# A two-layer cross network on Trainium2: layer 1 multiplies by x after the matmul instead of before it

## The reference

```python
e = stack([tbl_f[ids[:, f]] for f in range(32)], axis=1)    # (512, 32, 32)
prev = x0 = e
for W in (filter_0, filter_1):     # (1, 32*32, 128), (1, 32*128, 128)
    z = einsum('bhd,bmd->bhmd', x0, prev).reshape(b, h * m, d)
    prev = relu(einsum('bpd,pn->bnd', z, W[0]))
    outs.append(prev)
z = sum(concatenate(outs, axis=1), axis=-1)                 # (512, 256)
h = relu(concatenate([z, dense_ctx], axis=1) @ W_top1 + b_top1)
h = relu(h @ W_top2 + b_top2)
y = h @ W_top3
```

## Time and profile before

| | us |
|---|---|
| median of 3 runs | 1014.08 (1012.17 to 1014.36) |
| span of the profiled execution | 1007.7 |
| median less span | 6.4 |
| PE busy | 926.3 |
| DVE busy | 900.1 |
| POOL busy | 799.1 |
| ACT busy | 494.0 |
| mean granted clock of TensorE | 0.995 |

### The profile page before, as it was taken

How to read it: one execution, slowest core, us unless ns; L and a number is a source line. 1 busy time by engine, 2 the same in 40 slices (tenths; PEclk the granted TensorE clock), 3 DMA queues, 4 the chain that set the end, 5 groups by cost and what they waited for, 6 DMA issues and landing times.

```text
span 1007.7 us, 11260 instructions
## 1 busy us (share of the span) xinstructions
PE 926.3 (92%) x3132; PEld 590.2 (59%) x3132; DVE 900.1 (89%) x750; ACT 494.0 (49%) x606; POOL 799.1 (79%) x461
## 2 busy tenths in 40 slices
PE   0168899999999999999999999999999999999998
PEld 0125466666656666666656666666666666666664
DVE  0128999999899999999899999999999999999971
ACT  0224555556455545556445455556555555454531
POOL 6727988987997999987997999987877767777760
PEclk9999999999999999999999999999999999999999
DMA  8178556555565555555564555455555545555100
GB/s 230 37 218 263 172 182 186 180 185 162 142 197 167 191 183 186 165 179 172 154 195 157 190 191 186 145 193 171 163 193 183 193 162 187 184 159 172 42 0 0
DMA packets 58645, 166.70 MB, mean 165 GB/s; under 512 B 9649, under 2 KB 23185, under 8 KB 50466
## 3 DMA queue, kind: packets, MB, share of 16 engines
q1 hardware_dynamic: 51602, 160.62, 49.2%
q0 software_dynamic: 4096, 2.11, 1.5%
q10 hardware_dynamic: 2928, 3.76, 1.2%
HBM read 129.75 MB, written 5.24 MB: 134 GB/s over the span
## 4 chain that ended last, share of the span: by engine, by line
PE 61%; issue 16%; DVE 14%; DMA 4%; ACT 4%; SPq 1%; DVEq 0%; ACTq 0%
PE acc L814 26%; PE acc L751 11%; PE acc L753 11%; PE acc L752 11%; DVE prod L692 7%; DVE lo L644 5%; ACT hi L509 3%; DMA prev_rep<-prev 2%; DVE prod L648 2%; DMA whole<-xt_scratch 1%; DMA ctx_in<-in_dense_ctx 1%; PE prev_ps L851 1%; ACT relu L574 1%; PE acc L766 0%; PE prod L843 0%
## 5 line engine op out<-in xcount | busy, mean ns | idle before, releaser
L406 POOL TENSOR_TENSOR whole<-xa,prev_rep 128x1024 f32<-128x1024 f32 x224 | 541.3, 2421 | 137.3 <-PE acc L814 115.2
L509 ACT ACTIVATE hi<-prod 128x1024 fp32r<-128x1024 f32 x352 | 360.5, 1026 | 392.4 <-DVE prod L692 250.4
L644 DVE TENSOR_TENSOR lo<-prod,hi 128x1024 fp32r<-128x1024 f32 x352 | 417.2, 1221 | 20.7 <-ACT hi L509 19.1
L814 PE MATMUL acc<-whole,w_whole 128*128 128x512 f32 x896 | 420.6, 592 | 0.0
L751 PE MATMUL acc<-hi,w_hi 128*128 128x512 f32 x704 | 367.7, 522 | 29.8 <-DVE lo L644 17.3
L692 DVE TENSOR_TENSOR prod<-xa,prev_ps 128x1024 f32<-128x1024 f32 x288 | 339.9, 1221 | 0.6
L753 PE MATMUL acc<-hi,w_lo 128*128 128x512 f32 x704 | 279.2, 397 | 0.0
L752 PE MATMUL acc<-lo,w_hi 128*128 128x512 f32 x704 | 276.5, 393 | 0.0
L814 PEld LDWEIGHTS acc<-whole,w_whole 128*128 128x128 f32 x896 | 168.9, 188 | 125.5 <-issue 107.6
L751 PEld LDWEIGHTS acc<-hi,w_hi 128*128 128x128 f32 x704 | 134.0, 190 | 113.8 <-issue 56.5
L752 PEld LDWEIGHTS acc<-lo,w_hi 128*128 128x128 f32 x704 | 134.3, 191 | 71.5 <-issue 50.4
(11 more groups left out here) (60 smaller groups left out, 204.3 us busy)
## 6 DMA issues: line engine op xcount, KB each, us to landing
xa<-xt_scratch SPq DMA_DIRECT2D x32, 2048.0 KB, 7.6
prev_rep<-prev SPq DMA_DIRECT2D x128, 256.0 KB
xb<-xt_scratch SPq DMA_DIRECT2D x30, 1024.0 KB
x<-xt_scratch SPq DMA_DIRECT2D x62, 192.0 KB
xm<-xt_scratch SPq DMA_DIRECT2D x31, 256.0 KB
xt_scratch<-xt_stage SPq DMA_DIRECT2D x7, 256.0 KB
whole<-in_L_rec_filter SPq DMA_DIRECT2D x18, 64.0 KB
xt_scratch<-xt_stage SPq DMA_DIRECT2D x9, 128.0 KB
```

Source lines behind the costliest of these rows:

```text
L406: pool.tensor_tensor(whole[:, k % R], xa[:, par, g:g + 2, :], prev_rep[:, par, j, None, :].to_broadcast([P, 2, C]), ALU.mult).then_inc(who ...
L509: act.activation(hi[:, slot], prod[:, n_prod % 2], ACT.Copy).then_inc(hi_ready, 1)
L644: dve.tensor_tensor(lo[:, slot], prod[:, n_prod % 2], hi[:, slot].bitcast(F32), ALU.subtract).then_inc(lo_ready, 1)
L814: mm = pe.matmul(acc1[:], w1_whole[:, m, u, :], whole[:, m % R, u, :], start=False, stop=m == WHOLES - 1 and u == 1)
```

## The change

Layer 1 is turned round. The stationary operand is now a slice of `prev` (128 maps m by the 128 examples of one d, `prev_hi` and `prev_lo`, split once per chunk from the PSUM of layer 0), and the moving operand is the filter of four fields at a time (`w1_hi`, `w1_lo`, 128 rows m by 4 fields times 128 outputs). The result has the examples on the partitions, and x[b, h, d] is one number per partition and field, which scales it afterwards.

A chunk has four tiles q (one d each), a tile has eight PSUM banks of four fields, and each bank is three fp32r matmuls. For four of the eight banks ("A", `bank_a`, PSUM `ya`, 2 banks) ACT scales each field's 128 columns from PSUM into `scaled` (`scale_bank`, four ACTIVATEs with a per-partition scale read from `emb`), and POOL adds the four banks up in two additions (`sum_tile`, 1024 and 512 columns). For the other four ("D", `bank_d`, PSUM `yd`, 3 banks) DVE multiplies and adds field by field onto a running sum in SBUF that starts from POOL's part (`add_bank`, four `scalar_tensor_tensor` of 128 columns). DVE then folds the sum over the last four fields and takes the relu and the sum over d (`finish_a`, `finish_b`, `finish_c`).

Nothing is replicated any more: `replicate_prev`, `xa`, `acc1`, the fp32 matmuls and the copies of `prev` to PSUM are gone. Layer 0 keeps its 13 matmuls, one K-tile at a time with one `prod` bank; `xm` is copied to PSUM by ACT (`copy_xm`), so that DVE's product has one operand there. DVE takes over `sum0`. The chunks are software-pipelined and written out, no longer in hardware loops: iteration c of eight slots runs `bank_a` of chunk c, `bank_d` of chunk c - 1 and layer 0 of chunk c + 1, and there are 33 iterations. Batch tile 1's first 16 gathers are ahead of the loop, the rest inside it, and `emb` has two slots. The core of the diff (removed code of the old layer 1 is shown only in part):

```diff
...
+    DB = 4
+    AB = F // HB - DB
+    A_FIELD = HB * DB
+    RD, RA = 3, 2
+    PR = 3
...
-        acc1 = psum("acc1", [P, C])
-        prev_ps = psum("prev_ps", [P, 2, C])
-        prod = psum("prod", [P, 2, 2, C])
+        prod = psum("prod", [P, C])
+        xm_ps = psum("xm_ps", [P, C])
+        yd = psum("yd", [P, RD, C])
+        ya = psum("ya", [P, RA, C])
         identity = sb("identity", [P, P])
...
-            def replicate_prev(q):
-                for j in range(J):
-                    part = prev[32 * j:32 * (j + 1), q, :]
-                    src = bass.AP(part.tensor, part.offset, [list(part.ap[0]), [0, 4], [1, C]])
-                    sp.dma_start(prev_rep[:, q, j, :], src).then_inc(prev_replicated[q][j], 16)
...
+            def sum_tile(c, q):
+                n = DC * c + q
+                pool.wait_ge(a_used, a_number(c, q, AB - 1) + 1)
+                if n > 0:
+                    pool.wait_ge(part_ready, n)
+                piece = scaled[:, n % PR, :]
+                pool.tensor_tensor(half[:], piece[:, 0:AB * C // 2], piece[:, AB * C // 2:AB * C], ALU.add).then_inc(halved, 1)
+                if c > 1:
+                    pool.wait_ge(d_used, d_number(c - 2, q, 0) + 1)
+                pool.wait_ge(halved, n + 1)
+                pool.tensor_tensor(part[:, c % 2, q].rearrange("p i n -> p (i n)"), half[:, 0:C], half[:, C:2 * C],
+                                   ALU.add).then_inc(part_ready, 1)
...
+            for c in range(CHUNKS):
+                some = gathers_of(c)
+                for q in range(DC):
+                    sum_tile(c, q)
+                    for bt, f in some[len(some) * q // DC:len(some) * (q + 1) // DC]:
+                        if f == 0 and bt >= 2:
+                            pool.wait_ge(d_used, DB * DC * CPB * (bt - 1))
+                        gather(bt, f, gathered[bt])
+                    if q == 0 and c + 1 < CHUNKS:
...
+            def split_high(c, k):
+                n = KT * c + k
                 act.wait_ge(product_ready, n + 1)
-                act.activation(hi[:, slot], prod[:, n_prod % 2], ACT.Copy).then_inc(hi_ready, 1)
+                if n > 1:
+                    act.wait_ge(split_used, n - 1)
+                act.activation(hi[:, n % 2, :], prod[:], ACT.Copy).then_inc(hi_ready, 1)
...
+            def prev_high(c):
...
+                act.activation(prev_hi[:, c % 3, :], acc0[:], ACT.Relu).then_inc(prev_hi_ready, 1)
+            def scale_bank(c, q, j):
+                n, tile = a_number(c, q, j), DC * c + q
+                act.wait_ge(a_ready, n + 1)
+                if j == 0 and tile >= PR:
+                    act.wait_ge(halved, tile - PR + 1)
+                for i in range(HB):
+                    op = act.activation(scaled[:, tile % PR, C * j + N * i:C * j + N * (i + 1)],
+                                        ya[:, n % RA, N * i:N * (i + 1)], ACT.Copy,
+                                        scale=scale_of(c, q, A_FIELD + HB * j + i))
+                op.then_inc(a_used, 1)
             act.wait_ge(gathered_first, 16 * EARLY)
...
+                for s in range(SLOTS):
+                    if turning and s == TURN_SLOT:
+                        stage_xt((c + TURN_LEAD) // CPB, 0)
+                        stage_xt((c + TURN_LEAD) // CPB, 1)
+                    for j in (2 * (s % 2), 2 * (s % 2) + 1):
+                        scale_bank(c, s // 2, j)
+                        if j % 2 == 0 and c + 1 < CHUNKS:
+                            if s < KT:
+                                split_high(c + 1, s)
+                            if s == KT:
+                                small_high(c + 1)
+                            if s == 6:
+                                prev_high(c + 1)
+                    if s == 5 and c + 2 < CHUNKS:
+                        copy_xm(c + 2)
...
+            def product(c, k):
+                n = KT * c + k
+                if k == 0:
+                    dve.wait_ge(xm_in_psum, c + 1)
+                    dve.wait_ge(xb_loaded, 16 * (c + 1))
+                if n > 0:
+                    dve.wait_ge(lo_ready, n)
+                dve.tensor_tensor(prod[:], xb[:, k, :], xm_ps[:], ALU.mult).then_inc(product_ready, 1)
...
+            def prev_low(c):
+                dve.wait_ge(prev_hi_ready, c + 1)
+                dve.scalar_tensor_tensor(prev_lo[:, c % 3, :], acc0[:], 0.0, prev_hi[:, c % 3, :].bitcast(F32),
+                                         ALU.max, ALU.subtract).then_inc(prev_lo_ready, 1)
...
+            def add_bank(c, q, j):
+                n = d_number(c, q, j)
+                dve.wait_ge(d_ready, n + 1)
+                if j == 0:
+                    dve.wait_ge(part_ready, DC * c + q + 1)
+                    if c > 1:
+                        dve.wait_ge(fin_a, c - 1)
+                else:
+                    dve.wait_ge(d_used, n - 1)
+                for i in range(HB):
+                    before = part[:, c % 2, q, i, :] if j == 0 else acc[:, c % 2, q, i, :]
+                    op = dve.scalar_tensor_tensor(acc[:, c % 2, q, i, :], yd[:, n % RD, N * i:N * (i + 1)],
+                                                  scale_of(c, q, HB * j + i), before, ALU.mult, ALU.add)
+                op.then_inc(d_used, 1)
...
+            def finish_a(c):
+                dve.wait_ge(d_used, DB * DC * (c + 1))
+                if c > 0:
+                    dve.wait_ge(fin_b, c)
+                dve.tensor_tensor(fold_a[:], acc[:, c % 2, :, 0:2, :], acc[:, c % 2, :, 2:4, :], ALU.add).then_inc(fin_a, 1)
...
+                dve.tensor_tensor(fold_b[:], fold_a[:, :, 0, :], fold_a[:, :, 1, :], ALU.add).then_inc(fin_b, 1)
...
+                    dve.scalar_tensor_tensor(sum1[:], fold_b[:], 0.0, sum1[:], ALU.max, ALU.add).then_inc(summed1, 1)
...
+            for c in range(CHUNKS + 1):
+                for s in range(SLOTS):
+                    pair, j = s // 4, s % 4
+                    if c > 0:
+                        add_bank(c - 1, 2 * pair, j)
+                    if c + 1 < CHUNKS:
+                        if s < KT:
+                            if s > 0:
+                                split_low(c + 1, s - 1)
+                            product(c + 1, s)
+                        if s == KT:
+                            split_low(c + 1, KT - 1)
+                            small_low(c + 1)
+                    if c > 0:
+                        add_bank(c - 1, 2 * pair + 1, j)
+                    if s == 5 and c > 1:
+                        finish_a(c - 2)
+                    if s == 6:
+                        if c + 1 < CHUNKS:
+                            prev_low(c + 1)
+                            add_to_sum0(c + 1)
+                    if s == 7 and c > 1:
+                        finish_b(c - 2)
+                        finish_c(c - 2)
+            finish_a(CHUNKS - 1)
...
+            def bank_a(c, q, j):
+                n, fields = a_number(c, q, j), slice(A_FIELD + HB * j, A_FIELD + HB * (j + 1))
+                pe.wait_ge(a_used, n - RA + 1)
+                three_passes(ya[:, n % RA, :], prev_hi[:, c % 3, P * q:P * (q + 1)], prev_lo[:, c % 3, P * q:P * (q + 1)],
+                             w1_hi[:, fields, :], w1_lo[:, fields, :], True, True).then_inc(a_ready, 1)
+            def bank_d(c, q, j):
+                n, fields = d_number(c, q, j), slice(HB * j, HB * (j + 1))
+                if n >= RD:
+                    pe.wait_ge(d_used, n - RD + 1)
+                three_passes(yd[:, n % RD, :], prev_hi[:, c % 3, P * q:P * (q + 1)], prev_lo[:, c % 3, P * q:P * (q + 1)],
+                             w1_hi[:, fields, :], w1_lo[:, fields, :], True, True).then_inc(d_ready, 1)
...
-                        mm = three_passes(acc1[:], w1_hi[:, k, u, :], w1_lo[:, k, u, :],
-                                          hi[:, s, u, :], lo[:, s, u, :], k == 0 and u == 0, False)
-                    mm.then_inc(split_used, 1)
-                    if k in WHOLE_AFTER:
-                        m = WHOLE_AFTER.index(k)
-                        pe.wait_ge(whole_ready, WHOLES * c + m + 1)
-                        for u in range(2):
-                            mm = pe.matmul(acc1[:], w1_whole[:, m, u, :], whole[:, m % R, u, :],
-                                           start=False, stop=m == WHOLES - 1 and u == 1)
-                        mm.then_inc(whole_free, 1)
...
+            for c in range(CHUNKS + 1):
+                turning = c + TURN_LEAD in [bt * CPB for bt in range(1, BT)]
+                if c < CHUNKS:
+                    pe.wait_ge(prev_hi_ready, c + 1)
+                    pe.wait_ge(prev_lo_ready, c + 1)
+                for s in range(SLOTS):
+                    if turning and s == TURN_SLOT:
+                        bt = (c + TURN_LEAD) // CPB
+                        pe.wait_ge(sorted_d, 2 + bt)
+                        turn_x(bt, 0)
+                        turn_x(bt, 1)
+                    for j in (2 * (s % 2), 2 * (s % 2) + 1):
```

(15 more changed lines are left out.)

748 lines of the change are left out of this document (267 added, 481 removed).

## The result

| | before | after | forecast |
|---|---|---|---|
| median of 3 runs, us | 1014.08 | 1162.16 (1161.77 to 1162.47) | 984 (945 to 1075) |
| span of the profiled execution | 1007.7 | 1160.7 | 977.6 |
| mean granted clock of TensorE | 0.995 | 0.919 | |

The ratio is 1.147, with an interval of 1.145 to 1.150: 15% slower, above the range. Ratios in this document leave out two slow executions of the kernel before that ran beside e5, e6, e8 and e9 (1224.7 and 2971.5 us, where the others have 1010 to 1016).

A forecast was written before the change was run, and what follows sets the result against it. PE and DVE together were taken to bound the 28.25 us chunk. Forecast: 71.5 + 18.5 + 31 x 26.8 + 18.8 + 26 + 9 + 3 = 977.6, plus 6.4, 984 us; range 945 to 1075.

The forecast's parts named there:

- DVE's four instructions with two SBUF operands: finish_a, finish_b, finish_c and small_low in each chunk: 3.0 us at quiet, 4.9 against POOL as before, 4.4 forecast.
- The term s: Time of one of DVE's 64 128-column scalar_tensor_tensor per chunk: taken as 0.24 us, between 0.20 and 0.26.
- the row of 286 ns: Profile row before the change: a 128-column DVE instruction with a per-partition scalar, cited for little pointer cost.
- The first rival: DVE's small instructions do not overlap, 0.26 us or more each; 1062 us at 0.28, 1088 at 0.293; chance 0.26.
- the break-even of 0.256: DVE small-instruction time in us at which the forecast equals the kernel before, 1014.1 us, with a chunk of 27.8.
- T: Time of one chunk of the loop: 28.25 us before, forecast 26.8 from DVE's 26.3 plus 0.5.
- the form of an open latency: First rival's worst form: memory latency lies open between short DVE instructions, 0.32 us each, 1142 us; chance 0.03.
- The coupling: Waits in a chunk between PE, DVE and ACT through the PSUM banks and ACT's split: 0.5 us per chunk.
- The 6.4 us carried over: Amount by which the median exceeds the profiled span, added to the forecast span of 977.6 us.
- Rival (2): PE becomes the chunk's bound, with DVE's small instructions near 0.20 us: PE's 25.1 plus 0.7, 953 us; chance 0.14.
- Rival (3): ACT and the hand-overs set the chunk: ACTIVATEs at 0.30 us, 0.4 wait per slot, 29.5 us, 1068; chance 0.12.
- The row of `lo` against `prod`: Profile rows on DVE before: lo, reading PSUM, lasts 1221 ns; a same-size product of two SBUF operands 1228.

The follow-up runs named there:

- e5: The change with finish_a moved on DVE to the end of slot 4 (was 5), finish_b and finish_c to slot 6 (was 7): 1019.8 us.
- e6: The change without the third matmul pass of each layer 1 bank on PE, 77 matmuls per chunk instead of 109: 1101.3 us.
- e8: The change with PSUM dealt out as 2 D banks and 3 A banks instead of 3 and 2: 1080.5 us.
- e9: The change with finish_a at the end of slot 4, finish_b and finish_c at the end of slot 1 of the next iteration: 1005.8 us.
- e1: The change with DVE's folds and the sum working on only 8 of every 128 outputs: 1038.7 us.
- e13: e9 with finish_a back at the end of slot 5, where the change has it: 1066.1 us.
- e2: The change with POOL adding only 32 columns in each of its two additions: 979.7 us.
- e14: e9 with small_low a bank later, finish_a before slot 1's second bank, finish_b and finish_c before slot 3's, POOL's finished-tile fold moved: 977.9 us.
- e3: The change with a constant instead of the pointer to x in DVE's 64 small instructions per chunk: 959.7 us.
- e12: e9 without the third matmul pass of layer 1 on PE, 77 matmuls per chunk instead of 109: 1005.4 us.
- e15: e14 with finish_a one slot earlier, behind slot 0's second bank, and finish_b and finish_c behind slot 3's second bank: 1031.4 us.

## Why the prediction was wrong

**The step that failed** is the price of DVE's four instructions with two SBUF operands. I took them at 4.4 us per chunk, from a mean of 1943 ns in the loop against 1228 at quiet, scaled by the share of time that POOL would be adding. That treats the collision as a slower stream, averaged over chance meetings. Neither holds: it is a wait for the rest of POOL's instruction (e1), and in a periodic chunk the meeting isn't chance, the same pair meets again (e5, e9, e13). `fold_a` alone was 1.9 us too long in each chunk; the four took 7.7 us, 3.3 over the forecast. Without the meetings they take 3.3 in all (e2), and by placing alone 3.8 (e14).

**The term s was mis-sized.** 0.26 us and not 0.24. The prediction had the right pieces, 0.20 by overlap and 0.06 for the pointer as ACT shows it, and then took the middle because of the row of 286 ns. e3 confirms both pieces; that row, with a plain SBUF source, says nothing about this instruction. 64 x 0.019 = 1.2 us per chunk. The first rival is thereby true in its mild form, and since 0.26 lies above the break-even of 0.256, the sign would have been lost by this alone: with s = 0.26 and all else as forecast T is 28.1 and the time about 1025. It isn't true in the form of an open latency: small instructions overlap, 0.26 from start to start at a record of 0.34.

**The coupling was too small.** It was 0.5 us per chunk, 0.9 with gathers and turns; 2.4 was measured. DVE waits 1.4 us per chunk for PE and 0.8 for ACT's `small_split`. The 0.8 had no term: `small_low` was taken to find its input ready. The 1.4 goes with the long folds: in e9, where they are short, the wait for PE is 20.1 / 32 = 0.6. Through what it goes, PE's stops or the lower clock behind them, is argued above and not shown apart.

The sum: 31 x (1.2 + 3.3 + 1.5) = 186 us on 984, less 5 for what lies around a span, is 1165 against 1162. The 6.4 us carried over were not what lies around a span: the change's profiled execution took 1162.47 us with a span of 1160.7, and one of the kernel before in a later run 1010.22 with 1008.1, about 2 us in both. The rest was a difference between executions.

**What held.** The loop was to start at 71.5: the first `prev_lo` starts at 71.7, and PE's first `ya` bank at 72.69. PE's fp32r matmuls are 0.23 apart. ACT's small ones are 0.26 apart, by eight in 2.17 us with a record of 0.38, as forecast. POOL's `half` is 2.40. ACT's wait for gathers is 13.0 us in three waits, where 9 was put down for two. PE waits more for DVE than for ACT, as said. Rival (2), PE as the bound, is not what happened, and e12 excludes it for e9 too. Rival (3), ACT, isn't either: ACT has 60% of its time filled and waits for others. Its T of 29.5 doesn't follow from its terms, since 22.8 and eight waits of 0.4 make 26.0; 29.5 is DVE's 26.3 with those waits. The row of `lo` against `prod`, which spoke against the Trainium skill's 58 and 120 cycles (VectorE: DVE Perf Modes, on the TRN2 errata), was borne out: with a PSUM source the constant form lasts 282 ns, no longer than the 293 of two SBUF operands. That the measured spacing of 0.259 meets the 258 ns of that estimate is chance: e3 has the same PSUM source and 0.20, and the difference is the pointer. Nor does the trace show the bubble per tile that the same page describes, between instructions that don't depend on each other.

**The rule that would have told it** was at hand. The Trainium skill (SBUF — State Buffer, on who interferes with whom) says that a DVE instruction with two SBUF inputs contends with a GpSimd instruction that reads SBUF, and (of DVE's two-port modes) that the holder of the shared ports blocks the other for its whole instruction. The fold of 64 columns that lasts 1.99 us agrees. Where the page has the order of issue decide who blocks, the trace agrees at 498.87 and 528.02 us of e15, and at 548.44 in the change. At 510.94 in the change DVE started 0.41 us ahead of `half` and was the one that stood, but POOL's gather had been running for 0.55 us. How a gather takes part is open: in e8 `fold_a` and `fold_b` start 0.6 to 0.7 us into a gather, `half` follows it in the same way, and they keep their length.

The collision was already in the trace of the kernel before, behind the mean of 1943 ns. Of those 62 products 28 last 1.22 or 1.23 us. The other 34 last 1.57 to 4.43, and each of them ends 1.09 or 1.10 us after one of POOL's additions, nearly a product's whole length. The longest stood behind two additions in a row:

```profile
507.73 4.43 DVE L648 TENSOR_TENSOR prod<-xb,xm 128x1024 f32<-128x1024 f32 x1
```

```profile
506.36 4.70 POOL L406 TENSOR_TENSOR whole<-xa,prev_rep 128x1024 f32<-128x1024 f32 x2
```

(The second row holds two additions, the last of which ends at 511.06; the product ends at 512.16.) This called for the timeline of both engines side by side, not for a ratio.

**The change itself** is then worth something: with nothing but DVE's order, and POOL's fold of a finished tile, moved it is 3.4% faster than the kernel before (e14), at 977.9 us. Its T of 27.2 is also the forecast's, by luck: there DVE's small instructions take 1.2 us more than forecast, the four 0.6 less, and what is left for waits is 0.6 less.

## What to carry to other kernels

Where two engines exclude each other, the one that comes second waits for the rest of the other's instruction. Price it so, up to a whole instruction, and place it in the repeating unit's timeline on both engines: a share of busy time gives the mean over all phases, and a periodic kernel has only one. Of the two, let the engine with time to spare come second. Any edit that changes the length of the unit moves all phases, so an experiment on something else (a bank count, a cheaper operand) can gain or lose tens of us by this alone; look at the mean lengths of the exposed instructions in each run before the time is put down to the edit. When a break-even lies inside the two values that a term may have, find the row for its exact kind of operand, or forecast the sign as open.

## What was not expected of the hardware

- A fold of 64 columns lasts 1.99 us inside a POOL addition of 2.39 (e1), where the same fold lasts 0.22 when it meets nobody (1008.91 us).
- Small instructions with one SBUF tensor, one PSUM tensor and a pointer keep their 0.34 us whatever POOL does (means of 339 to 346 ns in all runs that have the pointer).
- The pointer costs DVE 0.06 us per instruction, in the spacing and in the record (342 and 282 ns), the same as a bias pointer costs ACT.
- A gather that POOL starts while `fold_a` runs is held too: 0.95 us otherwise, 1.84 when it starts 0.23 us into the fold, and it ends 0.86 after it (e5, e9).
- Where a fold starts 0.55 us into a gather and `half` follows, the fold waits for `half` as well (3.9 us, in the change, e6 and e13). Why it doesn't in e8, 0.6 to 0.7 us into the gather, was not tested.
